# New instruction orders for the last Mamba slot and the routing, on four engines

## The chip, the cores and the metric

The kernel runs on one core of one Trainium2 chip. A core has five engines that each work through a queue of their own in order: TensorE (PE, matrix products into the PSUM banks), VectorE (DVE), ScalarE (ACT), GpSimd (POOL) and SyncE (SP), which here only issues transfers. They meet through semaphores: an instruction increments one when it ends, and another waits until it has reached a value. The metric is device time in microseconds (us) of one launch; lower is better.

## What is computed

Two layers of mixed blocks on x of 8 batches, 256 tokens and 128 features, all in float32. Cut to what matters:

```python
x = x + L0_attn(L0_cond(x))        # a stencil, then 4 Mamba layers, then a layer norm
x = x + L0_ffn(L0_cond2(x))        # an MLP with per-batch expert columns, then 8 experts, top 2 of each token
x = x + L1_attn(L1_cond(x))        # masked pooling, then 16-head causal attention
x = x + L1_ffn(L1_cond2(x))        # per-batch linear, then a ternary MLP

def mamba_block(x):                # per layer; state of 16 per channel, 256 channels
    dA  = exp(dt[..., None] * A)
    dBu = dt[..., None] * Bm[:, :, None, :] * xm[..., None]
    h   = scan(dA, dBu)            # h[t] = dA[t] * h[t-1] + dBu[t], along the tokens
    y   = einsum('blds,bls->bld', h, Cm) + xm * D_skip
    return (y * silu(z)) @ out_w
```

The change lies in the stretch between the last of the Mamba work and the start of the expert tiles: the last pair of batches of the fourth Mamba layer, the final layer norm, L0_cond2 (up, gelu, down), the gate's logits, the choice of two experts for each token, and the lists that say which token goes to which expert tile.

## The kernel before

The Mamba part runs in 16 slots, one for each of 4 layers and 4 pairs of batches. In a slot the two batches of the pair are called a and b, and the 16 states of each are cut in 8 chunks of 2 states, so that a piece of work is named by its kind, its batch and its chunk:

- `mul:a4` makes dt·x·B for a chunk, on DVE or POOL (lines L1642 and L1648), 128x1024 elements.
- `dA:a4` is ACT's exp into PSUM (L1623), four instructions; the two PSUM places for it alternate by the chunk's number, so dA of a chunk waits for the scan two chunks earlier.
- `scan:a4` is DVE's recurrence (L1661). It waits for mul and dA of its chunk.
- `C:a4` multiplies the state by C, on POOL (L1667), and waits for the scan.
- `sum:a4` adds the chunk to y in PSUM bank 5 with two products by the identity on PE (L1702), and waits for C. `gate:a` (DVE, L1770) then takes y of the batch; the first sum of batch b waits for it, since both use bank 5.

In the last slot two chunks of batch b are added to their neighbours on DVE instead of PE: `join:0` adds b0 to b1, `join:1` adds b4 to b5 (L1766, both inputs in SBUF). So there is no sum:b0 and no sum:b4; `sum:b1` waits for join:0 and `sum:b5` for join:1, and join:1 itself waits for C:b5. `Clast` is the last chunk's C product, on DVE (L1673). Then follow gatelast (L1770), `outlast` (PE, L1780) and `reslast` (DVE, L1791), which completes the last Mamba output.

Between these the queues hold the pieces that come after the Mamba part, as far as their inputs are ready: `lnc`, `sq`, `rs`, `sc` (`lnsc` on DVE), `lnt`, `fin` (layer norm of a group of 512 tokens), `up`, `gelu`, `down`, `rT` (L0_cond2 for a batch), `logits`, then `best`, `second`, `ranks`, `places`, `slots`, `columns`, `rows`, `list`, `total`, `spread`, `ahead`, `tiling`, `table`, `lists` (routing), and `fold`, `xt` and `spin` (products of two attention weights, x turned to tokens, and products that only keep PE busy). ACT has to load another function table whenever it goes from exp to gelu or back (`gelus`, `exps`), 1.28 us each.

What sets the order is four strings, one for each engine, that name the pieces in the order in which that engine's queue gets them. For the last slot they are PE_LAST, ACT_LAST, DVE_LAST and POOL_LAST; the function `last` walks through a string and calls the piece behind each name. The waits are in the pieces and stay the same whatever the order. After the strings come the tails: the expert tiles (whose first PE instruction is the transpose at L514, for which POOL has gathered the tokens by the list), the attention and the last MLP. The tails' orders are the same before and after.

Of the kernel before, what the change touches and what calls it, by code (L numbers as in the profile page):

```python
# [2560 lines left out]
back conv:0 sum:l6 sum:l7 z:0 conv:1 out sum:a0 sum:a1 sum:a2 z:1 xproj sum:a3 dt:0 sum:a4 dt:1 sum:a5 sum:a6 sum:a7  # L2561
lnc:0 sum:b0 sum:b1 sum:b2 sum:b3 lnt:0 lnc:1 sum:b4 sum:b5 lnt:1"""
PE_LAST = """
sum:l6 sum:l7 out up:0 up:1 sum:a0 down:0 sum:a1 sum:a2 down:1 sum:a3 sum:a4 up:2 sum:a5 up:3 sum:a6 down:2 down:3
lnc:2 sum:a7 logits:3 sum:b1 logits:0 lnt:2 sum:b2 up:4 sum:b3 sum:b5 sum:b6 sum:b7 up:5 outlast ranks:0 lnc:3 down:4 down:5
lnt:3 logits:1 up:6 up:7 ranks:1 down:6 down:7 logits:2 fold:0 rows:0 rows:1 rows:2 fold:1 rows:3 ranks:2 total:0
spread:0 list:0 fold:2 ahead:0 fold:3 list:1 tiling:0 list:2 list:3 xt:0 xt:1 xt:2 xt:3 spin:8"""
ACT_NEXT = """
xn dA:a2 dA:a3 silus xm:0 exps dA:a4 shift:0 dA:a5 dA:a6 res dA:a7 ucopy:b dA:b0 silus xm:1 shift:1 zs:0 zs:1 exps xd
dA:b1 dA:b2 dA:b3 sp_abs sp_exp sp_ln dA:b4 dA:b5 sq:0 dA:b6 rs:0 dA:b7 ucopy:n sc:0 dA:n0 sq:1 rs:1 sc:1 dA:n1"""  # L2570
ACT_LAST = """
dA:a2 dA:a3 dA:a4 gelus gelu:0 res ucopy:b gelu:1 exps dA:a5 dA:a6 shift:2 dA:a7 rT:0 rT:1 dA:b0 dA:b1 gelus gelu:2
shift:3 gelu:3 exps dA:b2 rT:2 dA:b3 rT:3 sq:2 ones:0 dA:b4 dA:b5 rs:2 sc:2 dA:b6 dA:b7 gelus gelu:4 gelu:5 sq:3 exps
rs:3 rT:4 rT:5 gelus gelu:6 gelu:7 rT:6 rT:7 silus rows:0 rows:1 rows:2 fold:0 sums:0 sums:1 fold:1 rows:3 sums:2 columns:0
fold:2 rexp:0 xt:0 xt:1 xt:2 xt:3 fold:3"""
DVE_NEXT = """
mul:a01 mul:a2 scan:a0 scan:a1 scan:a2 mul:a3 scan:a3 gate:l scan:a4 scan:a5 mul:a7 scan:a6 scan:a7 mul:b012 mul:b345
scan:b0 scan:b1 scan:b2 scan:b3 dt gate:a scan:b4 scan:b5 scan:b6 scan:b7"""
DVE_LAST = """
mul:a0 mul:a1 fin:0 mul:a2 scan:a0 scan:a1 gate:l scan:a2 fin:1 mul:a3 scan:a3 mul:a7 mul:b0 scan:a4 mul:b1 scan:a5  # L2580
scan:a6 scan:a7 scan:b0 mul:b2 scan:b1 mul:b3 mul:b4 mul:b5 join:0 scan:b2 scan:b3 gate:a scan:b4 scan:b5 fin:2
scan:b6 join:1 scan:b7 Clast best:0 gatelast second:0 reslast places:0 slots:0 slots:1 lnsc:3 fin:3 best:1 second:1
idb places:1 slots:2 columns:1 best:2 second:2 places:2 columns:2 spans slots:3 table lists"""
POOL_NEXT = """
C:l7 mul:a456 C:a01 C:a2 C:a34 C:a56 mul:b6 C:a7 mul:b7 C:b0 C:b12 C:b3 u C:b4 C:b56"""
POOL_LAST = """
C:l7 mul:a4 mul:a5 C:a0 mul:a6 C:a1 C:a2 C:a3 C:a4 mul:b6 C:a5 C:a6 C:a7 C:b0 C:b1 mul:b7 C:b2 C:b3 C:b4 C:b5 C:b6"""
LOGITS = ((0, 4, 8), (1, 8, 12), (2, 12, 16), (0, 0, 4))
CONSTS, LAP_CONSTS = 15, 9
ACT_COLUMNS, PLACED = 4, 57  # L2590
# [94 lines left out]
```

## Time and profile before

| | |
|---|---|
| three runs | 1265.45, 1267.08, 1270.23 us; median 1267.08 us |
| the profiled execution's own time | 1266.82 us |
| its span in the profile | 1265.0 us |
| mean granted TensorE clock | 0.997 |
| busy: PE, DVE, POOL, ACT | 97%, 87%, 85%, 82% of the span |
| the last slot and the routing | from about 759.6 to 855.8 us of the span |

The time of a run holds the span from the first to the last instruction and about 1.8 us around it. Busy shares are means over stages with different limits. The change touches only some 96 us of the span, so what matters is which engine is waited for in that stretch.

### The profile page before, as it was taken

What the parts mean: (1) busy time and instruction counts of PE and PEld (TensorE: products, weight loads), DVE (VectorE), ACT (ScalarE), POOL (GpSimd) and SP (SyncE); (2) the same over time, 40 slices, a digit from 0 to 9 for tenths busy, and PEclk for the clock granted to TensorE, in tenths of its full rate; (3) what the DMA queues carried; (4) which work ended last, traced back from release to release, by engine and by line L of the source; (5) the groups of instructions that cost most, each with busy time, mean ns of one, the idle gap of its engine ahead of it and who ended that gap; (6) DMA issues with size and microseconds to landing.
All of it is one profiled execution on the core that took longest, in us unless ns stands there. A gap on an engine that the chain in (4) does not pass through costs nothing.

```text
span 1265.0 us, 24140 instructions
## 1 busy us (share of the span) xinstructions
PE 1227.4 (97%) x7347; PEld 732.1 (58%) x7349; DVE 1096.3 (87%) x1639; ACT 1032.1 (82%) x2706; POOL 1074.1 (85%) x642
## 2 busy tenths in 40 slices
PE   8899999999999999999999999989999999999997
PEld 4443554554554554554554545669998566666666
DVE  3999999999999999999999999975566677787776
ACT  4888999899999898998898988763244888888895
POOL 5699999999999999999999999655542978887681
PEclk9999999999999999999999999999999999999999
DMA  5654464454463553453553555352322000000000
GB/s 188 271 229 162 184 247 163 195 221 165 188 241 152 210 220 155 198 232 153 214 224 144 210 220 154 111 169 64 83 73 45 25 15 25 26 27 23 7 10 14
DMA packets 49595, 178.88 MB, mean 141 GB/s; under 512 B 15673, under 2 KB 33501, under 8 KB 40925
## 3 DMA queue, kind: packets, MB, share of 16 engines
q1 hardware_dynamic: 47180, 172.85, 36.4%
q0 software_dynamic: 2304, 4.72, 1.7%
q8 instruction: 49, 0.80, 0.3%
q14 instruction: 62, 0.50, 0.1%
HBM read 169.89 MB, written 16.52 MB: 147 GB/s over the span
## 4 chain that ended last, share of the span: by engine, by line
PE 41%; DVE 30%; ACT 14%; issue 13%; POOL 1%; DVEq 1%; ACTq 0%; POOLq 0%
DVE h L1661 23%; PE banks L347 10%; ACT banks L1623 6%; PE banks L524 6%; DVE h L1642 5%; PE banks L1702 4%; PE banks L917 4%; PE banks L1024 3%; PE banks L535 3%; PE banks L967 3%; PE banks L1448 2%; ACT L1492 2%; ACT L1489 2%; ACT xm L1455 1%; ACT zs L1467 1%
## 5 line engine op out<-in xcount | busy, mean ns | idle before, releaser
L1661 DVE TENSOR_TENSOR_SCAN h<-banks,h 128x1024 f32<-128x1024 f32 x256 | 571.0, 2272 | 4.0 <-ACT banks L1623 1.6
L1667 POOL TENSOR_TENSOR h<-h,Cb 128x1024 f32<-128x1024 f32 (+2 forms) x140 | 498.6, 3603 | 11.8 <-DVE h L1661 10.0
L1623 ACT ACTIVATE banks<-dt,A_cur 128x255 f32<-128x255 f32 x1024 | 424.7, 464 | 43.7 <-DVE h L1661 41.1
L1702 PE MATMUL banks<-h,ident 128*128 128x512 f32 x860 | 402.7, 602 | 6.1 <-POOL h L1667 2.6
L1702 PEld LDWEIGHTS banks<-h,ident 128*128 128x128 f32 x860 | 155.3, 190 | 184.6 <-issue 154.2
L1648 POOL TENSOR_TENSOR h<-Bb,u 128x1024 f32<-128x1024 f32 (+1 forms) x76 | 249.3, 3281 | 1.9 <-DVE xs L1562 1.8
L1642 DVE TENSOR_TENSOR h<-Bb,banks 128x1024 f32<-128x1024 f32 (+2 forms) x101 | 172.0, 1717 | 0.9 <-ACT banks L1607 0.7
L960 POOL TENSOR_SCALAR h<-h 128x128 f32<-128x128 f32 x124 | 92.3, 761 | 32.1 <-DVE h L942 31.9
L1448 PE MATMUL banks<-xn,wF 128*128 128x512 f32 x256 | 113.0, 592 | 1.8 <-ACT xn L1440 1.8
L960 POOL TENSOR_SCALAR Cb<-Cb,h 128x128 f32<-128x128 f32 x124 | 99.2, 816 | 9.7 <-DVE h L942 9.5
L1448 PEld LDWEIGHTS banks<-xn,wF 128*128 128x128 f32 x256 | 47.9, 188 | 62.5 <-issue 60.2
L524 PE MATMUL banks<-Cb 128*128 128x128 f32 x624 | 76.5, 275 | 0.9 <-ACT Cb L572 0.9
L524 PEld LDWEIGHTS banks<-Cb 128*128 128x128 f32 x624 | 73.1, 192 | 1.5 <-ACT Cb L572 1.3
L347 PE MATMUL banks<-Bb,h 128*64 128x256 f32 x512 | 65.1, 383 | 0.0
L1745 ACT ACTIVATE h<-banks,CT 128x256 f32<-128x256 f32 x156 | 61.7, 471 | 0.0
L616 DVE TENSOR_TENSOR Cb<-Cb,banks 128x512 f32<-128x512 f32 x39 | 26.7, 685 | 35.9 <-PE banks L524 26.0
L936 ACT ACTIVATE h<-h 128x128 f32<-128x128 f32 (+1 forms) x128 | 56.6, 448 | 1.4 <-issue 0.9
L936 ACT ACTIVATE Cb<-Cb,h 128x128 f32<-128x128 f32 (+1 forms) x128 | 57.0, 454 | 0.0
L917 PE MATMUL banks<-h 64*128 64x128 f32 (+1 forms) x512 | 56.5, 340 | 0.2 <-DVE h L928 0.2
L1024 PE MATMUL banks<-Bb,h 128*64 128x256 f32 (+1 forms) x512 | 54.1, 332 | 0.3 <-DVE Bb L995 0.3
L928 DVE CUSTOM_DVE_ANT_0 h<-banks,Bb 128x128 f32<-128x128 f32 (+1 forms) x128 | 38.6, 352 | 17.5 <-PE banks L917 17.5
L707 POOL DMA_INDIRECT xm<-by_expert,Bb x32 | 31.4, 983 | 26.0 <-DVE Cb L718 10.4
(395 smaller groups left out, 2092.4 us busy)
## 6 DMA issues: line engine op xcount, KB each, us to landing
Cb<-scrX SPq DMA_DIRECT2D x32, 2048.0 KB, 7.1
Bb<-scrX SPq DMA_DIRECT2D x31, 2048.0 KB, 7.1
by_expert<-in_x SPq DMA_DIRECT2D x15, 576.0 KB
h<-in_L_ffn_w SPq DMA_DIRECT2D x2, 2048.0 KB, 8.8
by_expert<-Cb SPq DMA_DIRECT2D x39, 64.0 KB
h<-in_conv_w SPq DMA_DIRECT2D x4, 512.0 KB, 4.4
Bb<-scrX SPq DMA_DIRECT2D x2, 1024.0 KB, 5.6
scr<-Cb SPq DMA_DIRECT2D x3, 640.0 KB, 3.0
```

Of the source, the lines that this page charges most:

```text
L347: m = e.matmul(out[at], weights[:, at], source, start=start, stop=stop, skip_group_check=True)
L524: m = e.matmul(bank(2 * w + q)[:, c * P:(c + 1) * P], w_now[q][w][:, c * P:(c + 1) * P], xgT[k], start=True, stop=True)
L917: m = e.matmul(bank(o)[:, lo:lo + n], qT[r:r + HS, p, jc * P:(jc + 1) * P], kT[r:r + HS, p, 0:n], start=True, stop=True)
L936: m = e.activation(Pr[h % 8][:, lo:lo + n], Pr[h % 8][:, lo:lo + n], ACT.Exp, bias=negm[:, jc, h:h + 1], scale=-1.0, accum_out=sums[:, jc, ...
L960: m = e.tensor_scalar(Pr[h % 8][:, lo:lo + n], Pr[h % 8][:, lo:lo + n], inv[:, jc, h:h + 1], None, ALU.mult)
L1448: m = e.matmul(ps_F[half][:].rearrange("p (b l) -> p b l", b=2), wF[:, FC_TAP + k * 2 * P + half * P:FC_TAP + k * 2 * P + (half + 1) * P], ...
L1623: m = e.activation(ps_dA[c % 2][:, g, half, 1:S], dts[q][:, half, i * S + 1:(i + 1) * S], ACT.Exp, scale=A_cur[q][:, s:s + 1])
L1642: e.tensor_tensor(h[i][:, rows(cs), :, :], both(Bb[i], cs), u_rows(ps_u, cs), ALU.mult).then_inc(sem("mulv"), len(cs))
L1648: e.tensor_tensor(h[i][:, rows(cs), :, :], both(Bb[i], cs), u_rows(us[q][:, :, i * S:(i + 1) * S], cs), ALU.mult).then_inc(sem("mulp"), le ...
L1661: e.tensor_tensor_scan(chunk(i, c), ps_dA_flat[c % 2], chunk(i, c), 0.0, ALU.mult, ALU.add).then_inc(sem("scan"), 1)
L1667: e.tensor_tensor(h[i][:, rows(cs), :, :], h[i][:, rows(cs), :, :], both(Cb[i], cs), ALU.mult).then_inc(sem("hC"), len(cs) + (turned_ahead ...
L1702: m = e.matmul(bank(5), ident[:], h_flat[i][:, s * HALVES * S:(s + 1) * HALVES * S], start=(s == GROUP * first_sum(p, i)), stop=(s == NS - 1))
```

## The change

Four strings are replaced: the order of the same pieces in the last slot, on PE, ACT, DVE and POOL. The new strings come from a search over orders in which the products of TensorE were reckoned seven per cent longer than they are. No piece is added or taken away, no size, wait or buffer is changed, SP's queue is the same. Of the diff one string shows how it looks:

```diff
 POOL_LAST = """
-C:l7 mul:a4 mul:a5 C:a0 mul:a6 C:a1 C:a2 C:a3 C:a4 mul:b6 C:a5 C:a6 C:a7 C:b0 C:b1 mul:b7 C:b2 C:b3 C:b4 C:b5 C:b6"""
+C:l7 C:a0 mul:a4 mul:a5 C:a1 mul:a6 C:a2 C:a3 C:a4 mul:b6 C:a5 C:a6 mul:b7 C:a7 C:b0 C:b1 C:b2 C:b3 C:b4 C:b5 C:b6"""
```

**POOL**, second half of the last slot: L1667 is C of a chunk, L1648 is mul of a chunk. Before, from mul:a6 on:

```order
L1648 TENSOR_TENSOR h<-Bb,u 128x1024
L1667 TENSOR_TENSOR h<-h,Cb 128x1024 x4
L1648 TENSOR_TENSOR h<-Bb,u 128x1024
L1667 TENSOR_TENSOR h<-h,Cb 128x1024 x5
L1648 TENSOR_TENSOR h<-Bb,u 128x1024
L1667 TENSOR_TENSOR h<-h,Cb 128x1024 x5
L2178 TENSOR_SCALAR Cb<-Bb 128x128 x16
```

And now, from mul:a6 on:

```order
L1648 TENSOR_TENSOR h<-Bb,u 128x1024
L1667 TENSOR_TENSOR h<-h,Cb 128x1024 x3
L1648 TENSOR_TENSOR h<-Bb,u 128x1024
L1667 TENSOR_TENSOR h<-h,Cb 128x1024 x2
L1648 TENSOR_TENSOR h<-Bb,u 128x1024
L1667 TENSOR_TENSOR h<-h,Cb 128x1024 x8
L2178 TENSOR_SCALAR Cb<-Bb 128x128 x16
```

C:a0 has gone ahead of mul:a4 and mul:a5, and mul:b7 ahead of C:a7, C:b0 and C:b1. After mul:b7 there are now eight C products in a row (a7, b0 to b6); before there were five (b2 to b6).

**DVE**, batch b of the last slot: L1642 mul, L1661 scan, L1770 gate, L1766 join, L1673 Clast, L1865 fin, L2130 the first step of best:0. Before, from mul:b3 on:

```order
L1642 TENSOR_TENSOR h<-Bb,banks 128x1024 x3
L1766 TENSOR_TENSOR h<-h 128x1024
L1661 SCALAR_TENSOR_TENSOR h<-banks,h 128x1024 x2
L1770 TENSOR_TENSOR yz<-banks,zs 128x2x256
L1661 SCALAR_TENSOR_TENSOR h<-banks,h 128x1024 x2
L1865 SCALAR_TENSOR_TENSOR xs<-banks,lng,ypad 128x512
L1661 SCALAR_TENSOR_TENSOR h<-banks,h 128x1024
L1766 TENSOR_TENSOR h<-h 128x1024
L1661 SCALAR_TENSOR_TENSOR h<-banks,h 128x1024
L1673 TENSOR_TENSOR h<-h,Cb 128x1024
```

And now, from scan:a5 on:

```order
L1661 SCALAR_TENSOR_TENSOR h<-banks,h 128x1024 x5
L1642 TENSOR_TENSOR h<-Bb,banks 128x1024 x3
L1661 SCALAR_TENSOR_TENSOR h<-banks,h 128x1024 x2
L1770 TENSOR_TENSOR yz<-banks,zs 128x2x256
L1766 TENSOR_TENSOR h<-h 128x1024
L1661 SCALAR_TENSOR_TENSOR h<-banks,h 128x1024 x3
L1766 TENSOR_TENSOR h<-h 128x1024
L1661 SCALAR_TENSOR_TENSOR h<-banks,h 128x1024
L1673 TENSOR_TENSOR h<-h,Cb 128x1024
```

join:0 stood right behind mul:b5, ahead of scan:b2, and now stands behind scan:b3 and gate:a. join:1 stands between scan:b6 and scan:b7 in both. fin:2 has moved from between scan:b5 and scan:b6 to behind Clast. mul:b0, mul:b1 and mul:b2 now come before scan:a5.

**PE**, from the skip product (L1678) of batch b: L1702 sum, L1946 logits, L1853 lnt, L1883 up, L1813 lnc, L1780 outlast, L1976 and on ranks:0. Before:

```order
L1678 MATMUL banks<-xm,wS 128x256 x2
L1946 MATMUL banks<-wF,Bb 128x8 x4
L1853 MATMUL banks<-ident,xc 128x128 x4
L1702 MATMUL banks<-h,ident 128x512 x2
L1883 MATMUL banks<-xs,wF 128x256 x4
L1702 MATMUL banks<-h,ident 128x512 x8
L1883 MATMUL banks<-xs,wF 128x256 x4
L1780 MATMUL banks<-yz,wS 128x512 x2
```

And now, from sum:b1 on:

```order
L1678 MATMUL banks<-xm,wS 128x256 x2
L1813 MATMUL banks<-center_w,xs 128x128 x4
L1702 MATMUL banks<-h,ident 128x512 x4
L1946 MATMUL banks<-wF,Bb 128x8 x4
L1702 MATMUL banks<-h,ident 128x512 x2
L1853 MATMUL banks<-ident,xc 128x128 x4
L1702 MATMUL banks<-h,ident 128x512 x4
L1883 MATMUL banks<-xs,wF 128x256 x4
L1780 MATMUL banks<-yz,wS 128x512 x2
L1883 MATMUL banks<-xs,wF 128x256 x4
L1813 MATMUL banks<-center_w,xs 128x128 x4
```

lnc:2 has moved behind sum:b1. sum:b5 stands alone between logits:0 and lnt:2, where before sums b3, b5, b6 and b7 ran in one stretch. up:4 has moved from between sum:b2 and sum:b3 to between sum:b7 and outlast, and up:5 from ahead of outlast to behind it; lnc:3 now comes ahead of ranks:0.

On ACT sq:2, rs:2, sc:2 now stand together between dA:b6 and dA:b7, and shift:2 ahead of dA:a2. In the routing at the end DVE's fin:3 comes after slots:1, the copy `idb` comes last, and PE and ACT take the pieces of rows, fold, list and xt in another order; fold:3 now stands between xt:1 and xt:2.

## Rows read from the trace of the kernel before

**Rows 1.** The page: its span and the busy share of each engine.
```profile
span 1265.0 us, 24140 instructions
...
PE 1227.4 (97%) x7347; PEld 732.1 (58%) x7349; DVE 1096.3 (87%) x1639; ACT 1032.1 (82%) x2706; POOL 1074.1 (85%) x642
```

**Rows 2.** The chain that ended last, 735 to 870 us: start, us, what.
```profile
821.29 1.73 PE banks L1883 x8
...
824.77 0.70 DVE xs L1791
...
854.04 1.79 PE banks L723 x16
```

**Rows 3.** DVE's timeline: start, duration, instruction; in brackets idle time before and its releaser.
```profile
759.64 2.32 DVE L1642 TENSOR_TENSOR h<-Bb,banks 128x1024 f32<-128x1024 f32 x2
761.89 0.74 DVE L1865 SCALAR_TENSOR_TENSOR xs<-banks,lng,ypad 128x512 f32<-128x512 f32 x1
...
781.52 8.83 DVE L1661 TENSOR_TENSOR_SCAN h<-banks,h 128x1024 f32<-128x1024 f32 x4
...
793.59 3.45 DVE L1642 TENSOR_TENSOR h<-Bb,banks 128x1024 f32<-128x1024 f32 x3
796.98 3.36 DVE L1766 TENSOR_TENSOR h<-h 128x1024 f32<-128x1024 f32 x1
...
804.64 0.66 DVE L1770 TENSOR_TENSOR yz<-banks,zs 128x512 f32<-128x512 f32 x1
...
813.89 1.20 DVE L1766 TENSOR_TENSOR h<-h 128x1024 f32<-128x1024 f32 x1
...
817.32 1.23 DVE L1673 TENSOR_TENSOR h<-h,Cb 128x1024 f32<-128x1024 f32 x1
...
821.40 0.69 DVE L1770 TENSOR_TENSOR yz<-banks,zs 128x512 f32<-128x512 f32 x1 [1.44 <-PE banks L1702]
...
851.74 0.29 DVE L2218 CAST Bb<-banks 128x128 int32<-128x128 f32 x1 [1.57 <-PE banks L2074]
```

**Rows 4.** POOL's timeline of the same stretch.
```profile
757.68 6.87 POOL L1667 TENSOR_TENSOR h<-h,Cb 128x2048 f32<-128x2048 f32 x2 [0.43 <-issue]
...
785.29 11.65 POOL L1667 TENSOR_TENSOR h<-h,Cb 128x1024 f32<-128x1024 f32 x5
796.86 2.39 POOL L1648 TENSOR_TENSOR h<-Bb,u 128x1024 f32<-128x1024 f32 x1
...
814.05 3.24 POOL L1667 TENSOR_TENSOR h<-h,Cb 128x1024 f32<-128x1024 f32 x1 [1.80 <-DVE h L1661]
```

**Rows 5.** PE's timeline of the same stretch.
```profile
802.64 0.95 PE L1946 MATMUL banks<-wF,Bb 128*128 128x8 f32 x8
805.35 3.49 PE L1702 MATMUL banks<-h,ident 128*128 128x512 f32 x4 [1.75 <-DVE yz L1770]
...
810.35 0.63 PE L1853 MATMUL banks<-ident,xc 128*128 128x128 f32 x4
...
814.26 7.03 PE L1702 MATMUL banks<-h,ident 128*128 128x512 f32 x16
...
825.52 1.16 PE L1813 MATMUL banks<-center_w,xs 128*128 128x128 f32 x8 [0.36 <-DVE xs L1791]
...
832.07 4.08 PE L1883 MATMUL banks<-xs,wF 128*128 128x256 f32 x16
...
855.79 0.30 PE L514 MATMUL banks<-ident,Cb 128*128 128x128 f32 x1
```

**Rows 6.** ACT's timeline: one table load, then dA of two chunks.
```profile
778.53 1.28 ACT L1492 ACT_TABLE_LOAD   x1
779.82 3.26 ACT L1623 ACTIVATE banks<-dt,A_cur 128x255 f32<-128x255 f32 x8
```

**Rows 7.** Stretches of 2 us: busy PE, PEld, DVE, ACT, POOL; granted clock; DMA share, GB/s.
```profile
804.00:806.00 2.00, 0.65 (x1) 0.50 (x2) 2.00 (x3) 1.49 (x5) 2.00 (x2) 0.75 0.85 195
806.00:808.00 2.00, 2.00 (x3) 0.67 (x2) 2.00 (x2) 1.94 (x9) 1.69 (x2) 0.50 1.01 375
```

More of the change, by code:

```diff
@@ L2563 @@
 PE_LAST = """
[L2564 to L2567, printed above, removed]
+sum:l6 sum:l7 out up:0 sum:a0 up:1 sum:a1 down:0 down:1 sum:a2 sum:a3 sum:a4 up:2 sum:a5 sum:a6 sum:a7 up:3 logits:3
+down:2 down:3 sum:b1 lnc:2 sum:b2 sum:b3 logits:0 sum:b5 lnt:2 sum:b6 sum:b7 up:4 outlast up:5 lnc:3 ranks:0 down:4
+down:5 lnt:3 logits:1 up:6 up:7 ranks:1 down:6 down:7 logits:2 rows:0 rows:1 fold:0 list:0 fold:1 rows:2 ranks:2
+total:0 spread:0 rows:3 ahead:0 fold:2 list:1 tiling:0 list:2 list:3 xt:0 xt:1 fold:3 xt:2 xt:3 spin:8"""
 ACT_NEXT = """
@@ L2571 @@
 ACT_LAST = """
[L2572 to L2575, printed above, removed]
+shift:2 dA:a2 dA:a3 dA:a4 res gelus gelu:0 ucopy:b gelu:1 exps dA:a5 rT:0 dA:a6 rT:1 dA:a7 dA:b0 dA:b1 shift:3 dA:b2
+dA:b3 gelus gelu:2 gelu:3 exps dA:b4 rT:2 dA:b5 rT:3 ones:0 dA:b6 sq:2 rs:2 sc:2 dA:b7 gelus gelu:4 gelu:5 sq:3 exps
+rs:3 rT:4 rT:5 gelus gelu:6 gelu:7 rT:6 rT:7 silus rows:0 fold:0 rows:1 rexp:0 rows:2 sums:0 fold:1 sums:1 rows:3
+sums:2 columns:0 fold:2 xt:0 xt:1 xt:2 xt:3 fold:3"""
 DVE_NEXT = """
@@ L2579 @@
 DVE_LAST = """
[L2580 to L2583, printed above, removed]
+mul:a0 mul:a1 fin:0 scan:a0 mul:a2 fin:1 scan:a1 gate:l scan:a2 mul:a3 scan:a3 mul:a7 scan:a4 mul:b0 mul:b1 mul:b2
+scan:a5 scan:a6 scan:a7 scan:b0 scan:b1 mul:b3 mul:b4 mul:b5 scan:b2 scan:b3 gate:a join:0 scan:b4 scan:b5 scan:b6
+join:1 scan:b7 Clast fin:2 best:0 gatelast second:0 reslast places:0 slots:0 lnsc:3 slots:1 fin:3 best:1 second:1
+places:1 slots:2 columns:1 best:2 second:2 places:2 columns:2 spans slots:3 table lists idb"""
 POOL_NEXT = """
```

## The prediction

> **What bounds the kernel now.** I read the page first: four engines are busy for 82 to 97% of the span, an average over stages that says nothing of this change [rows 1]. The change touches one stretch, so I went to the chain of waits there [rows 2] and then to the timelines of DVE, POOL, PE and ACT [rows 3 to 6], with the granted clock in short stretches [rows 7]. The reader should see three things.
>
> First, DVE sets the pace up to Clast. It begins mul:a0 at 759.64 and Clast at 817.32, almost without a gap, and most of that is scans (8.83 us for four, so 2.2 each) and muls (2.32 for two; records overlap by some 0.08, so 1.12 each) [rows 3]. One of its records is out of line: join:0 took 3.36 us, join:1 for the same work 1.20 [rows 3]. join:0 began at 796.98, right after POOL had begun mul:b7 at 796.86, which ended at 799.2; from there to 800.3 are the 1.1 us that a join needs. The other way round, POOL's C:b6 began 0.16 us after join:1 and took 3.24 where five C products before it took 11.65, or 2.31 each [rows 4]. So a join and a product on POOL run one after the other, and the one that has begun first goes first.
>
> Second, from gate:a on PE had a queue. It waited 1.75 us for gate:a, then its clock was granted at 0.50 from 805 to past 808, and the first sum took 3.49 us for a work that takes 1.72 elsewhere [rows 5, 7]. The last sums ran back to back until 821.29, some 3 us after Clast's end, and gatelast waited 1.44 for them [rows 2, 3, 5]. Then up:5 (1.73) and outlast (1.73) ran before reslast could start at 824.77 [rows 2].
>
> Third, from reslast to the first transpose of the expert tiles at 855.79 there is a chain of short steps over PE, ACT and DVE [rows 5]; what comes earlier at its head comes earlier at its end, if nothing else is late.
>
> **The change, step by step.** No work is added, so each engine's sum stays; only waits change. I take the new order with the old durations, and begin where the old trace still holds: DVE at 759.64, POOL at the end of C:l7, 764.5 [rows 3, 4].
>
> POOL: C:a0 waits for scan:a0, now behind two muls, fin:0 (0.66) and the scan: 759.64 + 2.24 + 0.66 + 2.2 = 764.75. Up to C:b1 there are 15 products, 15 x 2.31, without a wait, as DVE is ahead of each: C:b1 ends at 799.5, C:b2 at 801.85.
>
> DVE: ahead of join:0 now stand 11 muls (12.3), 12 scans (26.4), two fins (1.3) and two gates (0.6 each, 1.2), 41.2 us, and 0.1 of waiting for dA:a5, since ACT now has two gelus and two table loads (1.28 each) ahead of it [rows 6]: 801.0. sum:a7 ends at about 796.8, as C:a7 is done by 794.9, so gate:a no longer waits and PE no longer waits for it: before sum:b1 it has up:3, logits:3, down:2 and down:3 to do, to 802.8. join:0 waits for C:b2 and runs from 801.85 to 803.0. PE's wait of 1.75 us and the slow clock behind it are gone here; this is worth some 3.3 us of PE's time.
>
> The next step takes most of it back. From 803.0 DVE has scans b4, b5 and b6, 6.6 us, to 809.6. POOL has C:b3, held up by join:0, then C:b4 and C:b5, 3 x 2.31 = 6.9, to 809.9, and goes on at once with C:b6, whose scan is done. join:1 needs C:b5 and finds POOL 0.05 us into C:b6. It is released at 812.2 and ends at 813.35. Behind it on DVE wait scan:b7 (dA:b7 is ready at 811.2 in spite of sq:2, rs:2 and sc:2 ahead of it), to 815.6, and Clast, to 816.8. On PE sum:b5 waits for join:1, and behind it lnt:2 (0.47), sum:b6 and sum:b7: 813.4 + 3 x 1.72 + 0.47 = 819.0 [rows 5]. Old: 821.29 [rows 2]. That is 2.3 us earlier.
>
> up:4 then stands between sum:b7 and outlast, as up:5 did, and hides gatelast (0.6): reslast starts at 819.0 + 3.46 + 0.05 = 822.5. But up:5 is behind outlast now and lnc:3 behind that: lnc:3 runs from 824.2, where it ran from 825.52 [rows 5]. So 1.3 us are left. From there to up:6 the steps are the old ones; slots:1 ahead of fin:3 costs nothing, since lnt:3 waits for down:5 on PE until about then (cover gone, it would cost its 1.18). up:6 starts at 830.8 instead of 832.07 [rows 5]. In the lists the new order saves ACT 0.2 us before list:3, so DVE's lists (851.74 before) gain that; but PE has fold:3 (0.95) behind list:3 now, where it ran earlier, and the spin of 1.79 behind it [rows 2, 3]. The first transpose then hangs on PE's spin and not on the list: 0.2 us are lost. idb behind lists (0.3 us) is hidden by POOL's gather, which takes over 3 us from the end of lists to 855.79.
>
> Sum: 1.3 - 0.2 = 1.1 us earlier, and the tails are unchanged. Bounds: no gain at all at one end, and 4.7 at the other (all of PE's time saved, 821.29 less 816.6, the end of sum:b7 if join:1 had never waited). The sum stands against the profiled execution's own 1266.82 us, so 1265.7; the median of the runs is 0.26 above it, so I say 1266.0.
>
> **A rule against it.** PE's new wait before sum:b5 is 813.4 - 810.8 = 2.6 us, behind logits:0, whose eight narrow products fill little. In the old trace logits:3 and 1.75 us of idleness came just before the granted clock fell from 1.00 to 0.50, that is from 2.4 to 1.2 GHz [rows 5, 7]. The Trainium skill ("TensorE: Matmul & The Clock Gate", Part 1) says that the clock is granted by how busy the engine has been of late, so that the change would only move the slow stretch; the trace agrees in its one case. By the row alone the forecast has 1.1 us of gain with the clock up; by the rule it has the rival below.
>
> **The rivals.**
> A. join:1 gets in ahead of C:b6. It misses by 0.3 us on my count, after 45 us of adding up; if DVE is that much later or POOL earlier, join:1 runs at once. Then scan:b7 waits for dA:b7 at 811.1 and sum:b7 ends at 816.9, lnc:3 starts 3.4 earlier, and 3.1 us are left: 1264.0.
> B, the other side. The clock falls in the wait before sum:b5. Then that sum takes 3.49 instead of 1.72, all behind it on PE is 1.7 later, and 1.1 - 1.7 = 0.6 us are lost: 1267.7. It decides from the point where the slow stretch costs PE more than the 1.1. For it: the wait is longer than the old one. Against: PE is dense before it.
> C. join:0 comes after 801.85, finds C:b3 begun and waits to 804.15. Everything behind is 2.3 later: 1268.2. Against: 0.85 us of margin.
> D. Nothing moves at the end, because something else there is as late (the gather, the w1 and wo transfers): 1267.1. Little speaks for it; these hang on y of the last slot or on the lists, which are earlier too.
>
> **How the numbers follow.** The forecast 0.36, A 0.24, B 0.22, C 0.08, D 0.10. The likeliest one's own range is 1265.2 to 1266.8. From A to C is 1264.0 to 1268.2; with the scatter of the runs, some 1.5 us to the low side and 1 to the high side, 1262.6 to 1269.0. A measurement of this kernel can tell about 0.5%, 6.3 us, from no change. No case reaches it; I leave 0.04 for faster and 0.03 for slower, for what I have not seen.
>
> **What would show it.** Right: join:0 at about 801 with 1.9 to 2.1 us, and no wait of PE for gate:a; join:1 with 3.5 us or so and C:b6 beside it with 2.3; PE idle some 2.6 us before the sum ahead of lnt:2; sum:b7's end near 819; L514 near 854.7. Wrong: join:1 at 1.2 us and C:b6 at 3.2 (A); a granted clock of 0.5 after 811 (B); join:0 over 4 us (C). The prediction falls altogether if gate:a is still waited for, or if L514 comes more than 3.5 us earlier or any later than 857.

## The result, and the profile after

The changed kernel takes 1272.65 us (median of 20 runs, 1266.93 to 1277.74), the kernel before 1268.8 us beside it (20 runs, 1263.79 to 1275.03). The ratio is 1.0028, with a 95% interval of 1.0015 to 1.0041: slower by some 3.6 us by the ratio (3.85 by the medians), which the runs can tell from nothing, and less than 0.5%. The forecast was 1266.0 us, 1.1 us faster than before.

The profiled execution of the changed kernel is the second fastest of its 20: 1266.98 us, where that of before had 1266.82. The page, with its span, the busy engines, and the group of the sums (busy, mean ns | idle before, releaser and its part):

```profile
span 1265.2 us, 24140 instructions
...
PE 1224.2 (97%) x7347; PEld 729.9 (58%) x7349; DVE 1098.9 (87%) x1639; ACT 1032.3 (82%) x2706; POOL 1073.3 (85%) x642
...
L1702 PE MATMUL banks<-h,ident 128*128 128x512 f32 x860 | 401.6, 600 | 10.8 <-DVE h L1766 4.4
```

Busy times are those of before within 3.2 us [rows 1]; the order moved waits. The page names join as the main releaser of the sums. DVE's timeline in the stretch (start, duration, instruction, in brackets idle before and its releaser); L1770 at 800.09 is gate:a, L1766 the joins:

```profile
800.09 0.67 DVE L1770 TENSOR_TENSOR yz<-banks,zs 128x512 f32<-128x512 f32 x1
800.67 3.86 DVE L1766 TENSOR_TENSOR h<-h 128x1024 f32<-128x1024 f32 x1
804.46 6.64 DVE L1661 TENSOR_TENSOR_SCAN h<-banks,h 128x1024 f32<-128x1024 f32 x3
811.51 3.35 DVE L1766 TENSOR_TENSOR h<-h 128x1024 f32<-128x1024 f32 x1 [0.42 <-POOL h L1667]
814.79 2.28 DVE L1661 TENSOR_TENSOR_SCAN h<-banks,h 128x1024 f32<-128x1024 f32 x1
817.10 1.22 DVE L1673 TENSOR_TENSOR h<-h,Cb 128x1024 f32<-128x1024 f32 x1
...
820.95 0.69 DVE L1770 TENSOR_TENSOR yz<-banks,zs 128x512 f32<-128x512 f32 x1 [0.55 <-PE banks L1702]
...
851.76 0.29 DVE L2218 CAST Bb<-banks 128x128 int32<-128x128 f32 x1 [1.48 <-PE banks L2074]
```

POOL's timeline. The five are C:a7 and C:b0 to C:b3, the three C:b4 to C:b6:

```profile
791.82 11.63 POOL L1667 TENSOR_TENSOR h<-h,Cb 128x1024 f32<-128x1024 f32 x5
806.81 6.97 POOL L1667 TENSOR_TENSOR h<-h,Cb 128x1024 f32<-128x1024 f32 x3 [3.36 <-DVE h L1661]
```

PE's timeline: sum:b1, logits:0, sum:b5, then sum:b6 and sum:b7, up:4, lnc:3, up:6, and the first transpose of the expert tiles:

```profile
804.68 1.95 PE L1702 MATMUL banks<-h,ident 128*128 128x512 f32 x4 [2.02 <-DVE h L1766]
...
811.66 0.95 PE L1946 MATMUL banks<-wF,Bb 128*128 128x8 f32 x8
815.01 1.96 PE L1702 MATMUL banks<-h,ident 128*128 128x512 f32 x4 [2.40 <-DVE h L1766]
...
817.24 3.60 PE L1702 MATMUL banks<-h,ident 128*128 128x512 f32 x8
820.68 1.89 PE L1883 MATMUL banks<-xs,wF 128*128 128x256 f32 x8
...
825.85 1.05 PE L1813 MATMUL banks<-center_w,xs 128*128 128x128 f32 x8
...
832.59 4.09 PE L1883 MATMUL banks<-xs,wF 128*128 128x256 f32 x16
...
855.96 0.27 PE L514 MATMUL banks<-ident,Cb 128*128 128x128 f32 x1
```

What the reader is to see. mul:a0 starts at 758.79 here and at 759.64 before [rows 3], so 0.85 us are to be taken off before's times when positions are compared. gate:a runs without a wait, as forecast, and PE reaches sum:b1 early. But join:0, which began at 800.67, took 3.86 us, and not the 2.0 forecast. POOL's five products have no gap in them and end at 803.45; 2.3 us before that, at 801.1, C:b3 began, although join:0 had been waiting since 800.67. join:0 ended 1.1 us after C:b3. So the product that POOL had next went ahead of a join that was already waiting. join:1 then met C:b6, begun 0.05 us before, and took 3.35, as forecast. PE stood idle for 2.02 and 2.40 us, and the transpose comes 97.17 us after mul:a0, where it came after 96.15.

The granted clock in stretches of 2 us (busy PE, PEld, DVE, ACT, POOL; clock; DMA share, GB/s), around PE's second wait:

```profile
812.00:814.00 2.00, 0.61 (x6) 0.52 (x5) 2.00 (x1) 1.98 (x4) 1.78 (x1) 1.00 0.00 0
814.00:816.00 2.00, 0.99 (x3) 0.54 (x4) 2.00 (x2) 0.16 (x1) 0.00 (x0) 1.00 0.00 0
816.00:818.00 2.00, 2.00 (x9) 1.10 (x8) 1.97 (x2) 0.00 (x0) 0.00 (x0) 1.00 0.04 8
```

The clock stays at 1.00, that is 2.4 GHz, here and in the whole stretch, although PE is busy for 0.61 and 0.99 us of two of these pieces. The trace of before held a slow stretch, at 0.50, behind its wait for gate:a [rows 5, 7], and another at 44 to 48 us of the span, which the trace after hasn't either. So these two traces differ by the joins, and by two falls of the clock that only the one of before has. The early one probably has its part in mul:a0's 0.85 us; eleven of the twelve profiles below hold it, with mul:a0 at 759.05 to 760.69.

### The profile page after: what moved, and what is told of

It is laid out like the page before. It is cut to its first block, busy times and chain, and to the rows that moved or that the text cites. A ratio compares the mean times of both kernels' runs of the same rounds, so it can differ in the third digit from the quotient of the medians.

```text
span 1265.2 us, 24140 instructions
## 1 busy us (share of the span) xinstructions
PE 1224.2 (97%) x7347; PEld 729.9 (58%) x7349; DVE 1098.9 (87%) x1639; ACT 1032.3 (82%) x2706; POOL 1073.3 (85%) x642
## 4 chain that ended last, share of the span: by engine, by line
PE 39%; DVE 27%; issue 14%; ACT 14%; POOL 4%; DVEq 1%; DMA 0%; POOLq 0%; ACTq 0%
DVE h L1661 21%; PE banks L347 10%; ACT banks L1623 6%; PE banks L524 5%; DVE h L1642 4%; PE banks L917 4%; PE banks L1024 3%; POOL h L1667 3%; PE banks L535 3%; PE banks L1702 3%; PE banks L967 3%; PE banks L1448 2%; ACT L1489 1%; ACT L1492 1%; ACT xm L1455 1%
## 5 line engine op out<-in xcount | busy, mean ns | idle before, releaser
L1661 DVE TENSOR_TENSOR_SCAN h<-banks,h 128x1024 f32<-128x1024 f32 x256 | 571.4, 2275 | 4.5 <-ACT banks L1623 2.1
L1667 POOL TENSOR_TENSOR h<-h,Cb 128x1024 f32<-128x1024 f32 (+2 forms) x140 | 500.3, 3626 | 10.0 <-DVE h L1661 8.2
L1702 PE MATMUL banks<-h,ident 128*128 128x512 f32 x860 | 401.6, 600 | 10.8 <-DVE h L1766 4.4
L1702 PEld LDWEIGHTS banks<-h,ident 128*128 128x128 f32 x860 | 154.4, 190 | 189.9 <-issue 157.8
L1648 POOL TENSOR_TENSOR h<-Bb,u 128x1024 f32<-128x1024 f32 (+1 forms) x76 | 251.9, 3315 | 1.9 <-DVE xs L1562 1.8
L1642 DVE TENSOR_TENSOR h<-Bb,banks 128x1024 f32<-128x1024 f32 (+2 forms) x101 | 172.0, 1720 | 0.1
```

Of the source, the lines that this page charges most:

```text
L1642: e.tensor_tensor(h[i][:, rows(cs), :, :], both(Bb[i], cs), u_rows(ps_u, cs), ALU.mult).then_inc(sem("mulv"), len(cs))
L1648: e.tensor_tensor(h[i][:, rows(cs), :, :], both(Bb[i], cs), u_rows(us[q][:, :, i * S:(i + 1) * S], cs), ALU.mult).then_inc(sem("mulp"), le ...
L1661: e.tensor_tensor_scan(chunk(i, c), ps_dA_flat[c % 2], chunk(i, c), 0.0, ALU.mult, ALU.add).then_inc(sem("scan"), 1)
L1667: e.tensor_tensor(h[i][:, rows(cs), :, :], h[i][:, rows(cs), :, :], both(Cb[i], cs), ALU.mult).then_inc(sem("hC"), len(cs) + (turned_ahead ...
L1702: m = e.matmul(bank(5), ident[:], h_flat[i][:, s * HALVES * S:(s + 1) * HALVES * S], start=(s == GROUP * first_sum(p, i)), stop=(s == NS - 1))
```

## The experiments

Each was timed in five rounds beside the kernel before, in three groups, each group on one chip. Before took 1268.34 us beside the first four kernels (35 runs), 1264.0 beside the next four (30) and 1264.15 beside the last four (31). Ratios are to the same runs of before; they are the estimates on record and not the quotients of two medians, from which they differ by up to 0.0013 (e12: 0.9961 against 0.9974). The groups lie up to 5 us from the runs beside the result, so that an expectation that names a median under 1272.65 can only be read by its ratio. **L** is the time from mul:a0 to lists in the profiled execution: 92.10 before [rows 3], 92.97 after. From lists to the transpose pass 4.0 to 4.2 us, but 4.8 to 5.1 in e1, e2, e3, e6 and e8, where PE waits 0.4 to 0.9 us for the gathered tokens. Where lines were put into a kernel, those behind them read 2 or 3 higher (in the kernels with a guard L1768 is the join, L1669 C, and L1650 POOL's mul in e7 and e12).

Every run has its mean granted clock, and that explains most of the scatter: one straight line through all 250 runs, with a level for each kernel and chip and a common slope, gives 1.05 us (0.96 to 1.14) for 0.001 of mean clock. **Equal** is a kernel's level at clock 1.000 less that of before on its chip, good to about 1 us. The runs of before beside the result carry no clock of their own, so the changed kernel itself has no such figure.

| kernel | ratio | interval | mean clock | equal, us | joins, us | L, us |
|---|---|---|---|---|---|---|
| after | 1.0028 | 1.0015 to 1.0041 | 0.9963 | | 3.86, 3.35 | 92.97 |
| e1 guard0 | 1.0012 | 0.9994 to 1.0031 | 0.9962 | +1.2 | 1.48, 3.36 | 92.52, one fall |
| e2 guard01 | 0.9983 | 0.9965 to 1.0002 | 0.9978 | -0.5 | 1.33, 1.23 | 89.08 |
| e3 no joins | 1.0011 | 0.9995 to 1.0027 | 0.9963 | +1.3 | none | 91.90 |
| e4 filled | 1.0012 | 0.9996 to 1.0027 | 0.9979 | +2.2 | 3.81, 3.35 | 92.95 |
| e5 new routing | 1.0002 | 0.9992 to 1.0013 | 0.9959 | -0.6 | 3.36, 1.20 | 91.94, one fall |
| e6 new slot | 1.0028 | 1.0014 to 1.0042 | 0.9962 | +3.6 | 3.15, 3.35 | 97.82, two falls |
| e7 before, guard | 0.9967 | 0.9955 to 0.9980 | 0.9985 | -1.5 | 1.22, 1.20 | 91.81, one fall |
| e8 before, filled | 0.9986 | 0.9976 to 0.9997 | 0.9976 | -0.2 | 3.37, 1.19 | 90.65 |
| e9 join:0 first | 1.0014 | 0.9998 to 1.0029 | 0.9964 | +2.6 | 4.19, 3.35 | 93.58 |
| e10 guard1 | 0.9993 | 0.9980 to 1.0007 | 0.9975 | +0.5 | 3.98, 1.23 | 91.07 |
| e11 guard01 again | 0.9974 | 0.9962 to 0.9987 | 0.9979 | -1.6 | 1.46, 1.23 | 88.94 |
| e12 before, guard again | 0.9961 | 0.9944 to 0.9978 | 0.9985 | -1.3 | 1.22, 1.20 | 89.13 |

Of before, L without a fall is 90.65 (e8, whose joins are before's own); with its fall it is 92.10. The changed kernel's own difference, without a fall on either side, is thus 92.97 - 90.65 = 2.3 us.

**e1 and e2: POOL made to wait for the joins.** A guard in POOL's product makes C:b3 wait until join:0 has ended (e1), and C:b6 until join:1 has too (e2). DVE signals a join's end in `dA0`.

```diff
         def pool_C(e, p, q, i, *cs):
+            if isinstance(p, int) and p == LAST and i and cs[0] in {3: 3, 6: 4}:   # e1: {3: 3}
+                e.wait_ge(sem("dA0"), {3: 3, 6: 4}[cs[0]])
```

> The changed kernel, and in POOL's queue one wait more: C:b3 waits until join:0 is done. Theory 1 (a join that waits for POOL's product in progress is overtaken by POOL's next product): join:0 takes at most 2.0 us instead of 3.86, sum:b1 starts some 2.3 us earlier, join:1 still takes about 3.4 because C:b6 begins first, and the median is 1.5 to 3 us under the changed kernel's 1272.65. Theory 2 (the clock's falls on TensorE alone make the kernel slower): join:0 and the time of a run at a mean clock of 1.000 (1266.95 for the changed kernel) stay as they are.

> The changed kernel, and in POOL's queue two waits more: C:b3 waits for join:0, C:b6 for join:1. Theory 1: join:0 at most 2.0 us, join:1 about 1.2, sum:b7 ends 4 to 5 us earlier than in the changed kernel, L514 some 3.5 to 4.5 us earlier, PE hardly waits for a join; median 1267 to 1269, under both kernels in the time of a run at clock 1.000 (near 1263). Theory 2: the joins' records shorten but the time at clock 1.000 stays within 0.5 us of 1266.95.

e1 took 1268.43 us (12 runs). In its profile, DVE's joins, POOL's C products, and PE's sum:b5 with what follows it, to up:4:

```profile
802.01 1.48 DVE L1768 TENSOR_TENSOR h<-h 128x1024 f32<-128x1024 f32 x1
...
810.60 3.36 DVE L1768 TENSOR_TENSOR h<-h 128x1024 f32<-128x1024 f32 x1 [0.40 <-POOL h L1669]
```

```profile
793.07 9.34 POOL L1669 TENSOR_TENSOR h<-h,Cb 128x1024 f32<-128x1024 f32 x4
803.57 9.31 POOL L1669 TENSOR_TENSOR h<-h,Cb 128x1024 f32<-128x1024 f32 x4 [1.16 <-DVE h L1768]
```

```profile
814.11 2.78 PE L1704 MATMUL banks<-h,ident 128*128 128x512 f32 x4 [2.41 <-DVE h L1768]
...
817.53 4.09 PE L1704 MATMUL banks<-h,ident 128*128 128x512 f32 x8
821.46 1.89 PE L1885 MATMUL banks<-xs,wF 128*128 128x256 f32 x8
```

join:0 began 0.4 us before the end of C:b2 (793.07 + 9.34 = 802.41) and ended 1.1 after it: 1.48 instead of 3.86. POOL waited 1.16 us for it. That is the forecast's own step, and it happens only if POOL is held back. But in the 2.41 us wait before sum:b5 the clock then fell, and sum:b5 took 2.78 us and the two behind 4.09 (after: 1.96 and 3.60, behind a wait of 2.40 without a fall). From sum:b5 to up:4 it is 7.35 us here and 5.67 in after, so this fall costs 1.68 and L without it is 90.84:

```profile
814.00:816.00 2.00, 1.89 (x4) 0.93 (x5) 2.00 (x1) 0.00 (x0) 0.00 (x0) 0.78 0.04 8
816.00:818.00 2.00, 2.00 (x7) 1.25 (x6) 1.61 (x3) 0.00 (x0) 0.00 (x0) 0.50 0.00 0
818.00:820.00 2.00, 2.00 (x5) 0.83 (x4) 1.77 (x7) 0.00 (x0) 0.00 (x0) 0.87 0.00 0
```

e2 took 1266.07 us (12 runs): with both joins at 1.3 and 1.2 us L is 89.08, 3.9 less than after, and PE waits only 0.28 us before sum:b5. The transpose is 3.1 us earlier than in after, less than the 3.5 to 4.5 expected, as PE here waits for the tokens behind lists.

**e3: no joins.** All eight chunks of batch b are summed on PE.

```diff
-JOINED = ((1, 0), (1, 4))
+JOINED = ()
-down:2 down:3 sum:b1 lnc:2 sum:b2 sum:b3 logits:0 sum:b5 lnt:2 ...
+down:2 down:3 sum:b0 sum:b1 lnc:2 sum:b2 sum:b3 logits:0 sum:b4 sum:b5 lnt:2 ...
```

> The changed kernel without the two joins: sum:b0 and sum:b4 are on PE again (1.72 us each), DVE is free of join:0 and join:1. Theory 1: DVE loses 3.86 and 3.35 us of records, scan:b7 ends some 6 us earlier, PE gets 3.4 us more and becomes what is waited for; L514 2.5 to 4 us earlier than in the changed kernel. Theory 2: PE is busier in the waits, so falls get rarer, but the time at clock 1.000 gets longer by up to 3.4 us.

It took 1269.20 us (12 runs). DVE's scans b4 to b6, and b7:

```profile
803.98 6.66 DVE L1661 TENSOR_TENSOR_SCAN h<-banks,h 128x1024 f32<-128x1024 f32 x3 [1.45 <-ACT banks L1623]
814.13 2.29 DVE L1661 TENSOR_TENSOR_SCAN h<-banks,h 128x1024 f32<-128x1024 f32 x1 [3.49 <-ACT banks L1623]
```

DVE has no join left and waits 1.45 and 3.49 us for ACT's dA instead; L is 91.90, 1.1 less than with two blocked joins and 2.8 more than with two free ones; with one blocked (90.84 in e1 without its fall, 91.07 in e10) it is still less than with none. The expectation missed: scan:b7 ends 2.1 us earlier and not 6, as ACT is then waited for, and the transpose comes 0.5 us earlier than in after and not 2.5 to 4.

**e4 and e8: PE kept busy in its waits.** Idle products of 128x128, into columns that nobody reads, stand ahead of the waits for the joins (e4, after: 8 and 8) and of the wait for gate:a (e8, before: 7).

```diff
+                for _ in range(8):
+                    e.matmul(bank(4)[:, 3 * P:4 * P] if c == 5 else bank(5, P), center_w[:], ident[:], start=True, stop=True)
                 e.wait_ge(sem("dA0"), JOINED.index((i, c - 1)) + 3)
```

> The changed kernel, with eight idle products (128x128) on PE ahead of sum:b1 and eight ahead of sum:b5, where PE waits 2.0 and 2.4 us for the joins. Theory 1: the joins and the time at clock 1.000 stay (within 0.5 us of 1266.95). Theory 2: the waits no longer make the clock fall, and the median comes down from 1272.65 by 2 us or more, with mean clocks of 0.998 and above. If the falls come from elsewhere, the median stays within 1 us.

> The kernel before with seven idle products on PE in the wait for gate:a, behind which the profile of before shows the granted clock at 0.50. If that fall comes from this wait: no fall near 805, the first sum takes 1.9 instead of 3.49 us, lists start 90.2 to 90.6 us after mul:a0 instead of 92.10, and the mean clock over the runs goes up from 0.9965 by 0.001 or more. If not, the fall is still there in half of the runs and nothing changes.

e4 took 1268.53 us and e8 1262.99 us (12 runs each). e4's L is that of after, as its joins are; its mean clock is 0.9979, just short of the 0.998 expected, where after has 0.9963, and its ratio is 0.0016 lower, though the intervals overlap and the two were not timed together. In e8 the slow stretch is gone, and the clock is 1.00 where before had 0.75 and 0.50 [rows 7]:

```profile
804.00:806.00 2.00, 1.89 (x14) 1.51 (x13) 2.00 (x3) 1.49 (x5) 2.00 (x2) 1.00 0.82 176
806.00:808.00 2.00, 2.00 (x8) 1.16 (x7) 2.00 (x2) 1.94 (x8) 1.71 (x2) 1.00 1.04 377
```

L is 1.45 us less, and the runs are 0.14% faster (0.03 to 0.24), which is 1.8 us by the ratio and 1.0 by the medians, for seven idle products. The mean clock is 0.9976 where before has 0.9967 beside it, a little less of a rise than expected. At equal clock the kernel is that of before (-0.2), so what it gains is the fall. This fall costs 1.45 us of L; those behind sum:b5 in e1 and e6 cost 1.68.

**e5 and e6: the routing's order alone, and the last slot's alone.** The strings are cut behind outlast (PE), sq:3 (ACT) and reslast (DVE); e5 takes before's pieces ahead of the cut and the new order behind it, e6 the other way round. PE's string in e5:

```diff
-sum:b7 up:5 outlast ranks:0 lnc:3 down:4 ... logits:2 fold:0 rows:0 rows:1 rows:2 fold:1 rows:3 ...
+sum:b7 up:5 outlast lnc:3 ranks:0 down:4 ... logits:2 rows:0 rows:1 fold:0 list:0 fold:1 rows:2 ...
```

> The kernel before with one part of the change: everything up to outlast and reslast in the old order, everything behind them (the routing) in the new one. Theory 1 (the joins behind POOL's products cost it all): lists start 26.5 to 27.5 us after reslast as before (26.97) and the median is within 1.5 us of before. Theory 3 (the routing's new order costs part): reslast to lists is 0.4 us longer or more, and the median 0.4 to 1 us above before.

> The other half alone: the new order up to outlast and reslast, the old one behind. Theory 1: join:0 takes 3.8 us and join:1 3.35, lists start some 92.5 us after mul:a0 when the clock does not fall, and the median is 2.5 to 3.5 us above before. Theory 3: half of the loss at most, 1 to 2 us above before.

e5 took 1264.45 us (one of its 12 executions, of 2523 us, was disturbed, and the fit leaves it out), e6 1268.46 us (11 runs). From reslast to lists e5 takes 26.78 us, before 26.97. Behind the old slot the routing's order is worth 0.2 us at lists and nothing at the transpose (96.14 after mul:a0, 96.15 before), so the slot's order holds the loss. Behind the new slot it does count: there the same stretch takes 27.44 with the new routing (after) and 28.18 with the old one (e6), where ranks:0 stands between up:5 and lnc:3 on PE. In e6, join:0 began behind the start of C:b3 (805.42 against 805.2, which is 802.82 + 4.67 - 2.31) and took 3.15, not the 3.8 expected: ahead of it PE had waited 2.11 us for a transfer of weights (0.65 in after), with a fall of the clock behind that, and together they made join:0 3.15 us later. And PE's wait before sum:b5 was followed by a fall:

```profile
819.04 3.20 PE L1702 MATMUL banks<-h,ident 128*128 128x512 f32 x4 [2.39 <-DVE h L1766]
```

With 3.15 ahead of join:0, 1.68 for this fall and 0.74 behind reslast, less the 0.71 by which join:0 is shorter, L is 4.86 longer than in after: that is the whole of its 97.82.

**e7: the old order with a guard.** POOL's mul:b7, which went ahead of join:0 by 0.12 us [rows 3, 4], waits until join:0 has ended.

```diff
         def pool_mul(e, p, q, i, *cs):
+            if isinstance(p, int) and p == LAST and i and cs[0] == 7:
+                e.wait_ge(sem("dA0"), 3)
```

> The kernel before, and in POOL's queue one wait more: mul:b7 waits until join:0 is done. Theory 1: join:0 1.2 us instead of 3.36, all of DVE behind it 2.1 us earlier; how much of that reaches lists depends on PE's queue behind gate:a, between 0.5 and 2 us; median up to 2 us under before. Theory 2 (only the clock counts): join:0 shortens, the median stays within 0.5 us.

It took 1260.71 us (8 runs) and is faster than before by more than the 2 us expected. join:0 takes 1.22, and there is no slow stretch near 805; its profile has one between 774 and 778 us, behind a wait of PE of 2.60 us for a transfer of weights. L holds both: in e12 the wait is 1.38, the two pieces behind it take 4.11 us and not 5.54, and L is 2.7 less.

**e9: join:0 asks earlier.** If the margin had been too small, asking earlier would help.

```diff
-scan:a5 scan:a6 scan:a7 scan:b0 scan:b1 mul:b3 mul:b4 mul:b5 scan:b2 scan:b3 gate:a join:0 scan:b4 scan:b5 scan:b6
+scan:a5 scan:a6 scan:a7 scan:b0 scan:b1 mul:b3 mul:b4 mul:b5 scan:b2 scan:b3 join:0 gate:a scan:b4 scan:b5 scan:b6
```

> After, with join:0 put ahead of gate:a on DVE, so that it asks for its inputs at 800.0 us of the span (40.4 after mul:a0's start 759.6 in the profile after) instead of 800.67, while POOL is in the middle of C:b2. My theory (a waiting join is passed over by the product that POOL has queued, whenever it came): join:0 begins at about 41.2 after mul:a0, shows about 4.5 us and ends at the same 804.5; gate:a follows to 805.2, the scans behind are where they were, join:1 still 3.35, PE's sum:b1 0.7 later but that does not reach the end: as after, ratio to before 1.0028 (1.001 to 1.004). Rival (it was the margin: coming earlier it gets in behind C:b2): join:0 shows about 2.0 us, the scans of b4 to b6 end 1.6 us earlier, and the time is 1.6 us or more below after's, ratio 1.0015 or less.

It took 1267.07 us (12 runs). DVE's join:0, gate:a, scans and join:1, and POOL's five C products up to C:b3:

```profile
801.01 4.19 DVE L1766 TENSOR_TENSOR h<-h 128x1024 f32<-128x1024 f32 x1
805.12 0.68 DVE L1770 TENSOR_TENSOR yz<-banks,zs 128x512 f32<-128x512 f32 x1
805.72 6.64 DVE L1661 TENSOR_TENSOR_SCAN h<-banks,h 128x1024 f32<-128x1024 f32 x3
812.77 3.35 DVE L1766 TENSOR_TENSOR h<-h 128x1024 f32<-128x1024 f32 x1 [0.42 <-POOL h L1667]
```

```profile
792.49 11.62 POOL L1667 TENSOR_TENSOR h<-h,Cb 128x1024 f32<-128x1024 f32 x5
```

C:b2 ended at 792.49 + 11.62 - 2.31 = 801.8, so join:0 asked 0.8 us before that (0.5 in after), and was passed over all the same: it ended 1.1 after C:b3. The margin is no help. I had missed that gate:a, now behind the join, no longer runs beside the wait for POOL: the scans are 0.6 later, and so is L (93.58). The ratio, 1.0014, even lies where the rival had it (1.0015 or less), and in its width it doesn't tell the two apart (0.9998 to 1.0029); the length of the join and L do.

**e10: a guard for join:1 alone.** The guard of e2 with only C:b6 in it (`{6: 4}`).

> After, with only POOL's C:b6 made to wait until join:1 has ended; join:0 stays as it is. My theory (each of the two lost turns costs its own 2.1 to 2.3 us in the stretch): join:0 3.8, join:1 1.2 to 1.3, gatelast and reslast about 2.1 earlier after mul:a0 than in after, lists at 90.9 where after has 92.97; ratio to before 1.001 (0.9995 to 1.0025). With both guards the lists came at 89.08, with join:0's alone at 92.52 with a fall of the clock inside. Rival (the two are not additive, Clast or PE's sums take the gain back): lists at 92.5 or later, ratio 1.002 to 1.003.

It took 1263.83 us (12 runs). The joins, lists, and C:b6 on POOL:

```profile
800.84 3.98 DVE L1768 TENSOR_TENSOR h<-h 128x1024 f32<-128x1024 f32 x1
...
811.80 1.23 DVE L1768 TENSOR_TENSOR h<-h 128x1024 f32<-128x1024 f32 x1 [0.41 <-POOL h L1669]
...
850.12 0.29 DVE L2220 CAST Bb<-banks 128x128 int32<-128x128 f32 x1 [1.48 <-PE banks L2076]
```

```profile
813.10 2.35 POOL L1669 TENSOR_TENSOR h<-h,Cb 128x1024 f32<-128x1024 f32 x1 [1.34 <-DVE h L1768]
```

join:0 at 3.98 and join:1 at 1.23; L is 91.07, 1.9 less than after, and of e2's 3.9 this is one half, the price of join:1. e1, the other half, has 90.84 without its fall, so join:0's is 2.1. The two add up to 4.0. The ratio, 0.9993, is a little under the expected range.

**e11 and e12: the two best once more, on one chip.** e11 is e2 again, and e12 is e7 again.

> The new order with both guards once more, beside the old order with the guard on POOL's mul:b7, on one chip, to tell which of the two is the better version. Joins 1.3 and 1.2, lists 89.1 after mul:a0. My theory (a join that is not passed over is all that the new order lacked): ratio to before 0.998, 0.9965 to 1.0. Rival (the new order is worse in something else too, a longer last stage): ratio 1.0 or above.

> The old order with POOL's mul:b7 waiting until join:0 has ended, once more. Join:0 1.2 instead of 3.36, join:1 1.2. My theory: the 2.1 us saved on DVE show as 2 to 4 us in the end, ratio to before 0.997 (0.9955 to 0.9985), and at or below the new order with both guards. Rival (the first measurement of it was the chip's drift): ratio 0.999 to 1.0005.

e11 took 1261.39 us (12 runs), e12 1260.92 us (8 runs). e11's joins and lists on DVE, and C:a7 to C:b2, then C:b3 to C:b5, on POOL:

```profile
801.11 1.46 DVE L1768 TENSOR_TENSOR h<-h 128x1024 f32<-128x1024 f32 x1
...
809.72 1.23 DVE L1768 TENSOR_TENSOR h<-h 128x1024 f32<-128x1024 f32 x1 [0.40 <-POOL h L1669]
...
848.05 0.29 DVE L2220 CAST Bb<-banks 128x128 int32<-128x128 f32 x1 [1.48 <-PE banks L2076]
```

```profile
792.15 9.35 POOL L1669 TENSOR_TENSOR h<-h,Cb 128x1024 f32<-128x1024 f32 x4
802.65 7.03 POOL L1669 TENSOR_TENSOR h<-h,Cb 128x1024 f32<-128x1024 f32 x3 [1.16 <-DVE h L1768]
```

e12's join:0 and lists, and POOL's mul:b7:

```profile
797.36 1.22 DVE L1768 TENSOR_TENSOR h<-h 128x1024 f32<-128x1024 f32 x1
...
849.17 0.29 DVE L2220 CAST Bb<-banks 128x128 int32<-128x128 f32 x1 [1.57 <-PE banks L2076]
```

```profile
798.66 2.36 POOL L1650 TENSOR_TENSOR h<-Bb,u 128x1024 f32<-128x1024 f32 x1 [1.34 <-DVE h L1768]
```

In both, POOL stands idle for a good microsecond until the join is over, and DVE is not later for that, as L shows. With its joins free the new order's L (88.94) is as good as the old order's (89.13); the intervals of the two ratios overlap, so neither is shown to be the better. The old order needs one guard for it and the new one two. e10 and e11 ran on one chip and differ only by join:0's guard: L is 2.1 us less, the level at equal clock 2.1 less (+0.5 and -1.6), the median 2.4 less, though the intervals of the two ratios just overlap. That is what the step which the forecast had wrong costs, in the trace and in the runs.

## Why the prediction was wrong

**The step that failed** is this one: "join:0 waits for C:b2 and runs from 801.85 to 803.0." That join:0 would meet C:b2 was right (forecast 41.4 us after mul:a0, 41.9 measured), and so was the join's own 1.1 us. Wrong was what follows C:b2. I had read "the one that has begun first goes first" in the rows [rows 3, 4] and took a waiting join to be next in line. In the trace before, POOL had nothing ready behind mul:b7, since C:b2 needs scan:b2, which stood behind the join on DVE; so no row there showed who goes next when POOL has another product ready. It is POOL: 3.81 in e4, 3.86 in after, 3.98 in e10 and 4.19 in e9 are each what was left of C:b2 (0.4, 0.5, 0.6 and 0.8 us), 2.31 for C:b3 and 1.1 for the join. With POOL held back the same join took 1.48, 1.33 and 1.46. The Trainium skill ("SBUF — State Buffer", Who interferes with whom) says that of two such instructions the one that is issued first has the ports for its whole length; it doesn't say what becomes of one that waits already. The rule and the traces agree only if the waiting join doesn't count as issued. What makes POOL win, by which part of the chip, was not tried.

**Rival C named the outcome and not the way.** Its sum, "everything behind is 2.3 later", is what happened; its condition, that join:0 comes after 801.85, was not met, and "0.85 us of margin" protected nothing, as e9 shows. With no margin needed, C deserved far more than 0.08.

**The size.** From mul:a0, I forecast the transpose at L514 to be 1.1 us earlier, and the trace has it 97.17 - 96.15 = 1.0 later. Of the 2.1 between them, at lnc:3 2.5 are there (forecast 64.6 us after mul:a0, 67.06 measured): 2.1 for the product that went ahead (e10 against e11), and 0.4 of small errors in the sum. The same 0.4 come back from lnc:3 to the transpose, where I had counted 0.2 lost and the trace gains 0.2. join:1's step held (3.5 forecast, 3.35 measured; PE's wait 2.6 forecast, 2.40 measured), and so did "gate:a no longer waits".

**The slow clock was credited and not charged.** The forecast counted before's fall (3.49 instead of 1.72 for the sum) as gone, which it is in the profile, and gave rival B, that the clock falls in the new wait, 0.22. The runs show that it was more than a rival: a wait of 2.39 to 2.45 us before sum:b5 was followed by a fall in e1 and e6, and not in after and e9, the same wait each time. Over its 20 runs after has a mean clock of 0.9963, no better than before has in its three groups (0.9960 to 0.9967), so the credit for the fall was not paid out in the runs. That it is the new waits that brought falls back is likely and not shown: e1, e6 and e9, with such a wait, have 0.9962 to 0.9964, and e2, e4 and e11, without or with it filled, 0.9978 and 0.9979, but e3, without it, has 0.9963 too. The profiled execution, at 1.000, was one of only two at that level. That is why 1266.98 beside 1266.82 hid the loss: the two falls that before's trace holds, 1.45 us in L and up to 0.85 at mul:a0, stood against the 2.3 by which the new order's L is longer without falls. That 2.3 is the difference of two prices: 4.0 for the two blocked joins of the new order, less 1.5 for the one of the old order (90.65 in e8, 89.13 in e12), less 0.2 by which the new order is shorter with all joins free (88.94 against 89.13). Put together: 2.3 us between L's without falls, against 3.6 by the ratio with an interval of 1.9 to 5.2, and +2.2 and +2.6 at equal clock for e4 and e9, which have the same blocked joins. The slot's order alone has +3.6 (e6), 1.3 more than 2.3: 0.7 of it is the old routing behind the new slot (28.18 against 27.44), and the rest is within what the fit can be wrong by. How often the clock falls in after's own two waits could not be counted, as only one execution of it has a trace.

**The base.** I built on the three runs shown, 1267.08; 20 runs of the same kernel gave 1268.8 and their own range is 11 us wide. The upper end of 1269.0 left 1 us for scatter, where the runs of after reach 5 us above their median. Some 1.7 us of the 6.65 between forecast and result are this, 2.1 the join, and of the rest, about 2.8, some 1.45 is before's fall, credited and not gained, and 1.4 no experiment settles: 1266.0 + 1.7 + 2.1 + 2.8 = 1272.6. Rival A did not come about, join:1 met C:b6 as forecast, and D fell with the first trace, where the transpose moved by 1.0 us.

## What to carry to other kernels

Where VectorE reads two inputs from SBUF while GpSimd has products queued, reckon that a waiting VectorE instruction gets in only when GpSimd's queue has a gap; here that held for askings up to 0.8 us ahead. Where that matters, give GpSimd a wait on the VectorE instruction, which made both orders faster here (0.9961 and 0.9974 of the time before), and check that GpSimd has the slack. Before comparing two traces, take the falls of TensorE's clock out of both, and read how the mean clock of the other runs stands to the profiled one's. A short wait of TensorE just ahead of a critical product can be filled with idle products that nobody reads; here seven of them gave 1.0 us by the medians and 1.8 by the ratio (0.4 to 3.0).

## What the runs showed of the hardware

- A join that began to wait 0.4 to 0.8 us before the end of a GpSimd product was passed over by the next product in all four profiles where one was queued without a wait (after, e4, e9, e10), and ran at once behind the same product in all three where that next one was held (e1, e2, e11), though there it had begun to wait only 0.3 to 0.4 us ahead.
- TensorE's granted clock fell to 0.50 (1.2 GHz) behind waits of 2.39 (e6) and 2.41 us (e1) and stayed at 1.00 behind waits of 2.40 (after) and 2.45 (e9) in the same place; in another place it fell behind waits of 1.75 (before) and 1.77 us (e5). The falls that could be priced cost 1.4 to 1.7 us each. The Trainium skill ("TensorE: Matmul & The Clock Gate", Part 1) says that how much of one kernel runs at the slow level is variable from run to run; the traces agree.
- 0.001 of a run's mean clock stands for 1.05 us of its time in this kernel, and two chips ran the kernel before at 1264.0 and 1264.15 us, two groups of runs elsewhere at 1268.34 and 1268.8. That is 0.3 to 0.4% for one and the same kernel, as much as this change makes, so only kernels that share a chip can be compared this closely.
